# Row maxima of the scores: one unit of each round gets them from ScalarE, and they are spread by DMA instead of TensorE

## The reference

```python
xn = layernorm(x)                                   # x is 4 x 1024 x 256
q, k, v = split_heads(xn @ Wq), *split(xn @ Wkv)    # 16 heads of 64
q, k = rope(q), rope(k)                             # on the first 32 of 64
sim = einsum('bhid,bhjd->bhij', q, k) * 64 ** -0.5
attn = softmax(sim, axis=-1)
out = einsum('bhij,bhjd->bhid', attn, v) -> b n (h d)
x = x + (out @ Wout + bout) + ffn(xn)               # ffn: FP4 blocks of 16, silu(gate) * up, down
```

## Time and profile before

| | |
|---|---|
| median of 3 runs | 1926.34 us (1925.79 to 1928.39) |
| profiled execution | 1927.98 us |
| its span, first to last instruction | 1926.2 us |
| TensorE busy | 1843.6 us, 96% |
| VectorE busy | 1482.3 us, 77% |
| ScalarE busy | 808.2 us, 42% |
| GpSimd busy | 1395.9 us, 72% |

### The profile page before, as it was taken

How to read it: one execution, slowest core, us unless ns; L and a number is a source line. 1 busy time by engine, 2 the same in 40 slices (tenths; PEclk the granted TensorE clock), 3 DMA queues, 4 the chain that set the end, 5 groups by cost and what they waited for, 6 DMA issues and landing times.

```text
span 1926.2 us, 29651 instructions
## 1 busy us (share of the span) xinstructions
PE 1843.6 (96%) x11172; PEld 1147.6 (60%) x11172; DVE 1482.3 (77%) x2032; ACT 808.2 (42%) x1078; POOL 1395.9 (72%) x688
## 2 busy tenths in 40 slices
PE   6989999959999999999999999999999999999989
PEld 5768999835555555555555555555555555555589
DVE  7969999887777777777777777777777777776254
ACT  4642333214444444444444444444444444444432
POOL 4764554407888888888888888888888888889900
PEclk9999999969999999999999999999999999999989
DMA  8550311110221131222223121221322112211474
GB/s 287 234 192 28 127 46 53 42 50 23 53 69 54 54 102 53 65 56 60 63 57 110 53 59 53 61 60 53 90 76 64 58 54 59 53 51 48 148 263 170
DMA packets 151423, 161.33 MB, mean 84 GB/s; under 512 B 43376, under 2 KB 107760, under 8 KB 151024
## 3 DMA queue, kind: packets, MB, share of 16 engines
q1 hardware_dynamic: 151280, 159.43, 26.3%
HBM read 100.14 MB, written 59.24 MB: 83 GB/s over the span
## 4 chain that ended last, share of the span: by engine, by line
PE 63%; DVE 21%; issue 6%; DMA 1%; POOL 1%; ACT 0%; SPq 0%; POOLq 0%; DVEq 0%
PE banks L1005 19%; PE banks L1025 13%; PE banks L948 11%; PE banks L982 9%; PE banks L1008 6%; DVE half_max L1079 3%; PE banks L1516 2%; DVE q_lo L1124 2%; DVE k_lo L1124 2%; PE banks L1034 2%; DVE h_scales L110 2%; DVE f_y L131 2%; DVE f_amax L109 1%; DVE f_y L134 1%; DVE h L583 1%
## 5 line engine op out<-in xcount | busy, mean ns | idle before, releaser
L1203 POOL TENSOR_TENSOR acc<-acc,prob 128x1024 f32<-128x1024 f32 x384 | 917.9, 2390 | 131.2 <-ACT prob L1242 102.3
L1079 DVE TENSOR_REDUCE half_max<-banks 128x2 f32<-128x1024 f32 x512 | 627.2, 1226 | 270.9 <-PE banks L982 270.9
L1242 ACT ACTIVATE prob<-banks 128x1024 f32<-128x1024 f32 x512 | 511.8, 1024 | 633.8 <-PE banks L1008 633.8
L1025 PE MATMUL banks<-prob,v 128*64 128x512 f32 x2048 | 495.7, 605 | 0.0
L1025 PEld LDWEIGHTS banks<-prob,v 128*64 128x64 f32 x2048 | 124.3, 136 | 238.6 <-issue 190.9
L1203 POOL TENSOR_TENSOR acc<-prob,prob 128x1024 f32<-128x1024 f32 x64 | 153.5, 2399 | 124.6 <-ACT prob L1242 124.6
L982 PE MATMUL banks<-k_hi,q_hi 64*128 64x512 f32 x1024 | 230.9, 450 | 12.1 <-DVE half_max L1079 11.0
L948 PE MATMUL banks<-xT,wqk 128*128 128x512 f32 x768 | 218.0, 420 | 3.5 <-DVE k_lo L1124 2.1
L1005 PE MATMUL banks<-q_hi,k_lo 64*128 64x512 f32 x1024 | 202.9, 393 | 0.0
L1008 PE MATMUL banks<-max_rows,ones_r 64*128 64x512 f32 x1024 | 202.8, 392 | 0.0
L1005 PE MATMUL banks<-q_hi,k_hi 64*128 64x512 f32 x1024 | 202.4, 392 | 0.0
(11 more groups left out here) (121 smaller groups left out, 2152.1 us busy)
## 6 DMA issues: line engine op xcount, KB each, us to landing
v_scratch<-v_out SPq DMA_DIRECT2D x32, 512.0 KB, 2.6
wqk<-wp_scratch SPq DMA_DIRECT2D x32, 512.0 KB, 3.6
v<-v_scratch SPq DMA_DIRECT2D x32, 512.0 KB, 4.7
inv_rows<-inv_scratch SPq DMA_DIRECT2D x128, 128.0 KB, 3.2
o_scratch<-o_norm SPq DMA_DIRECT2D x64, 256.0 KB, 2.1
o_in<-o_scratch SPq DMA_DIRECT2D x8, 2048.0 KB, 11.0
xn_scratch<-p_xT SPq DMA_DIRECT2D x32, 256.0 KB, 3.0
xT<-xn_scratch SPq DMA_DIRECT2D x8, 1024.0 KB, 6.3
```

Of the source, the lines that this page charges most:

```text
L1025: ins = nc.tensor.matmul(o_ps[head * DH:(head + 1) * DH, :], v[s % 2][:, kt, at:at + DH], prob[n % SLOTS][:, head, :], start=kt == 0, stop ...
L1079: nc.vector.tensor_reduce(half_max[:, half % 2, :, t % GRP, part], guess_bank(s, i), axis=AX.X, op=ALU.max, negate=True).then_inc(half_max ...
L1203: nc.gpsimd.tensor_tensor(acc[b][:, :, :], first, prob[n % SLOTS][:, :, :], ALU.add).then_inc(added, 1)
L1242: nc.scalar.activation(prob[n % SLOTS][:, :, :], s_ps[n % 2][:, :, :], ACT.Exp).then_inc(exp_done, 1)
```

## The change

- The transposition of the maxima leaves TensorE. `turn_max` is now VectorE's: a transpose of `max_cols` (now 128x32) in blocks of 32x32, behind `rotate` in rounds 3 and 7. Four small DMAs bring the parts together in DRAM in the order of the queries (`store_max`), and one DMA spreads the 1024 values of a half, both heads, to all 128 partitions of `max_all` (`spread_max`, 512 KB). `spread_rows`, the 0/1 table and its load go.
- Even units keep a pair of products for the maxima, now with a matrix whose row 0 (of each head) is one and whose others are zero, and `max_all` as the moving operand.
- Odd units have no such pair. ScalarE copies `max_all` into their two banks (`seed`) behind the exponential that empties them, and all six products add to what lies there (`start=False`).

```diff
@@ misc_table, begin, tensor @@
-            if r == 0 and 0 <= s < STEPS:
-                job("turn", s, 1)
-            if r == 4 and 0 <= s + 1 < STEPS:
-                job("turn", s + 1, 0)
...
-        elif before == "turn":
-            pe.wait_ge(rows_done, 2 * s + k + 1)
@@ scores @@
+            has_seed = kt % SEEDED_EVERY == 1
+            if has_seed:
+                pe.wait_ge(seeded, n // SEEDED_EVERY + 1)
+            elif n >= 2:
+                pe.wait_ge(exp_done, n - 1)
             if kt == 0:
-                pe.wait_ge(rows_done, 2 * s + half + 1)
-            if n >= 2:
-                pe.wait_ge(exp_done, n - 1)
-            elif n == 1:
-                pe.wait_ge(kept["h_high"], TILES)
+                pe.wait_ge(max_in[half], 16 * (s + 1))
...
-                    nc.tensor.matmul(s_ps[n % 2][:, head, :], left[rows, keys], right[rows, queries], start=k == 0, stop=False)
-            for head in range(2):
-                rows = slice(head * DH, (head + 1) * DH)
-                ins = nc.tensor.matmul(s_ps[n % 2][:, head, :], ones_r[rows, :], max_rows[half][rows, :], start=False, stop=True)
+                    ins = nc.tensor.matmul(s_ps[n % 2][:, head, :], left[rows, keys], right[rows, queries],
+                                           start=k == 0 and not has_seed, stop=k == 2 and has_seed, skip_group_check=has_seed)
+            if not has_seed:
+                for head in range(2):
+                    rows = slice(head * DH, (head + 1) * DH)
+                    ins = nc.tensor.matmul(s_ps[n % 2][:, head, :], first_row[rows, :], max_all[half][rows, head, :], start=False, stop=True)
@@ vector @@
-        def spread_rows(s, half):
-            dve.wait_ge(misc_done, job["turn", s, half] + 1)
...
+        def turn_max(s, half):
+            dve.wait_ge(max_done, 2 * s + half + 1)
             if s:
-                dve.wait_ge(scored, (s - 1) * UNITS + (half + 1) * QT)
-            nc.vector.tensor_tensor(max_rows[half][:, :].rearrange("p (t n) -> p t n", t=GRP),
...
+                dve.wait_ge(max_stored[half], 16 * QUAD * s)
+            nc.vector.transpose(max_turned[half][:, :].bitcast(F32), max_cols[half][:, :].bitcast(F32)).then_inc(max_turn, 1)
@@ the loop of vector @@
+                if r in (3, 7) and scoring(s + 1):
+                    turn_max(s + 1, r // 4)
@@ scalar @@
+        def seed(n):
+            s, u = divmod(n, UNITS)
+            if u % QT == 1:
+                act.wait_ge(max_in[u // QT], 16 * (s + 1))
+            if n == 1:
+                act.wait_ge(half_maxed, UNITS)
+            else:
+                act.wait_ge(exp_done, n - 1)
+            nc.scalar.activation(s_ps[n % 2][:, :, :], max_all[u // QT][:, :, :].bitcast(F32), ACT.Copy).then_inc(seeded, 1)
...
                     exponent(s * UNITS + 2 * r + 1)
+                    if s * UNITS + 2 * r + 3 < STEPS * UNITS:
+                        seed(s * UNITS + 2 * r + 3)
+                elif s == -1 and r == ROUNDS - 1:
+                    seed(1)
@@ sync @@
+        def store_max(s, half):
+            if s:
+                sp.wait_ge(max_in[half], 16 * s)
+            sp.wait_ge(max_turn, 2 * s + half + 1)
+            for k in range(QUAD):
+                sp.dma_start(io["max_scratch"][half, :, :, k * QROWS:(k + 1) * QROWS].rearrange("h t c -> (h t) c"),
+                             max_turned[half][k * QROWS:k * QROWS + 2 * GRP, :].bitcast(F32)).then_inc(max_stored[half], 16)
+        def spread_max(s, half):
+            sp.wait_ge(max_stored[half], 16 * QUAD * (s + 1))
+            if s:
+                sp.wait_ge(scored, (s - 1) * UNITS + (half + 1) * QT)
+            sp.dma_start(max_all[half][:, :, :].rearrange("p h c -> p (h c)").bitcast(F32),
+                         io["max_scratch"][half].rearrange("h t p -> (h t p)").partition_broadcast(P)).then_inc(max_in[half], 16)
@@ the loop of sync @@
+            if scoring(s):
+                store_max(s, 1)
             if scoring(s - 1):
                 spread_inverse(2 * (s - 1))
+            if scoring(s):
+                spread_max(s, 1)
...
                 store_o(2 * (s - 1))
+            if scoring(s + 1):
+                store_max(s + 1, 0)
+                spread_max(s + 1, 0)
             if scoring(s - 1):
                 spread_inverse(2 * (s - 1) + 1)
```

More of the change, by code:

```diff
@@ L836 @@
 HALVES = 2 * STEPS
+SEEDED_EVERY = 2
 def attention_part(nc, zones, banks, sem, io, kept, output):
@@ L851, in attention_part @@
     shuffled = [first(f"shuffled{i}", [P, GCOL], F32) for i in range(2)]
-    own = small("own", [P, GRP], F32)
     ones = small("ones", [P, QROWS], F32)
-    ones_r = small("ones_r", [P, P], F32R)
+    first_row = small("first_row", [P, P], F32R)
     half_max = small("half_max", [P, 2, 2, GRP, 2], F32)
-    max_cols = [small(f"max_cols{i}", [P, P], F32) for i in range(2)]
-    max_rows = [small(f"max_rows{i}", [P, GCOL], F32R) for i in range(2)]
+    max_cols = [small(f"max_cols{i}", [P, QROWS], F32R) for i in range(2)]
+    max_turned = [small(f"max_turned{i}", [P, QROWS], F32R) for i in range(2)]
     compact = small("compact", [P, 2, 2, GRP], F32)
@@ L869, in attention_part @@
     o_norm = [late(f"o_norm{i}", [P, GCOL], F32) for i in range(2)]
+    max_all = [late(f"max_all{i}", [P, 2, GCOL], F32R) for i in range(2)]
     bout = late("bout", [P, D], F32)
@@ L884, in attention_part @@
     res_stored, wp_stored, down_done = kept["res_stored"], kept["wp_stored"], kept["down_done"]
-    guessed, half_maxed, max_done, rows_done = sem("guessed"), sem("half_maxed"), sem("max_done"), sem("rows_done")
+    guessed, half_maxed, max_done, seeded = sem("guessed"), sem("half_maxed"), sem("max_done"), sem("seeded")
+    max_turn = sem("max_turn")
+    max_stored, max_in = [sem(f"max_stored{i}") for i in range(2)], [sem(f"max_in{i}") for i in range(2)]
     scored, exp_done, pv_done, added = kept["scored"], sem("exp_done"), kept["pv_done"], kept["added"]
@@ L1036, in column_sums @@
             ins.then_inc(misc_done, 1)
-        def turn_max(s, half):
-            begin(pe, "turn", s, half)
-            pe.wait_ge(max_done, 2 * s + half + 1)
-            nc.tensor.transpose(misc_ps[:, 0:P], max_cols[half][:, :], ident[:, :]).then_inc(misc_done, 1)
-        pe.wait_ge(cleared, 4)
+        pe.wait_ge(cleared, 6)
         for s in range(-2, STEPS + 1):
@@ L1064, in tensor @@
                     column_sums(s, 0)
-                if r == 0 and scoring(s):
-                    turn_max(s, 1)
-                if r == 4 and scoring(s + 1):
-                    turn_max(s + 1, 0)
     def vector(dve):
@@ L1131, in invert @@
             nc.vector.reciprocal(inv_compact[:, b, :, :], compact[:, b, :, :]).then_inc(inv_done, 1)
-        dve.wait_ge(cleared, 4)
-        dve.wait_ge(tables_in, 32)
+        dve.wait_ge(cleared, 6)
+        dve.wait_ge(tables_in, 16)
         rotate(0, K0)
@@ L1145, in vector @@
                     maximum(s + 1, 2 * r)
-                if r == 1 and scoring(s):
-                    spread_rows(s, 1)
-                if r == 5 and scoring(s + 1):
-                    spread_rows(s + 1, 0)
                 if r == 0 and scoring(s + 1) and s >= 0:
@@ L1402, in clear @@
     def clear(dve):
-        nc.vector.memset(max_cols[0][:, :], 0.0).then_inc(cleared, 1)
-        nc.vector.memset(max_cols[1][:, :], 0.0).then_inc(cleared, 1)
+        nc.vector.memset(max_cols[0][:, :].bitcast(F32), 0.0).then_inc(cleared, 1)
+        nc.vector.memset(max_cols[1][:, :].bitcast(F32), 0.0).then_inc(cleared, 1)
         nc.vector.memset(ones[:, :], 1.0).then_inc(cleared, 1)
-        nc.vector.memset(ones_r[:, :].bitcast(F32), 1.0).then_inc(cleared, 1)
+        nc.vector.memset(first_row[:, :].bitcast(F32), 0.0).then_inc(cleared, 1)
+        dve.wait_ge(cleared, 4)
+        for head in range(2):
+            nc.vector.memset(first_row[head * DH:head * DH + 1, :].bitcast(F32), 1.0).then_inc(cleared, 1)
     def first_loads(sp):
@@ L1414, in first_loads @@
         load_x(sp, 0, 1)
-        sp.dma_start(own[:, :], io["tables"][:, P + 2 * SEQ:]).then_inc(tables_in, 16)
         load_wqk(sp, 1)
@@ L1641, in shape_constants @@
             turn[head * DH + dim, 1] = sin[:, dim // 2] if dim % 2 == 0 else -sin[:, dim // 2]
-    own = (np.arange(P)[:, None] % DH == np.arange(GRP)[None, :]).astype(np.float32)
-    return np.concatenate([np.eye(P, dtype=np.float32), turn.reshape(P, 2 * SEQ), own], 1)
+    return np.concatenate([np.eye(P, dtype=np.float32), turn.reshape(P, 2 * SEQ)], 1)
 def kernel(L0_attn_queries, L0_attn_Wq, L0_attn_Wkv, L0_attn_Wout, L0_attn_bout, L0_ffn_w_gate, L0_ffn_w_up, L0_ffn_w_down):
@@ L1677 @@
     io["sum_scratch"] = nc.dram_tensor("sum_scratch", (2, 2, GCOL), F32).ap()
+    io["max_scratch"] = nc.dram_tensor("max_scratch", (2, 2, GRP, P), F32).ap()
     io["inv_scratch"] = nc.dram_tensor("inv_scratch", (2, 2, GCOL), F32).ap()
```

4 lines of the change are left out of this document (1 added, 3 removed).

## The result

The changed kernel takes **1844.01 us**, the median of 4 runs (1841.81 to 1845.23), against 1926.07 us (1924.23 to 1928.39) of the kernel before, run beside it: a ratio of 0.957, 95% interval 0.956 to 0.959. The forecast was 1845, from 1838 to 1872. The profiled execution took 1844.23 us with a span of 1842.5, so the span shrank by 83.7 us.

A forecast was written before the change was run, and what follows sets the result against it. TensorE, busy 199.04 of 200 us, and its turns with DVE bound attention. Thirty steps of 2.64 us (79.2) and 1.9 at the start gave −81: 1927.98 to 1846.9, forecast 1845 after the 1.64 offset from the median, range 1838 to 1872.

The forecast's parts named there:

- Max products of odd units: On TensorE, eight pairs a step dropped at 0.2325 us each: 1.86 us a step saved.
- the tie: Round 0: the second guess's result reaches DVE at 2.40 us, the rotary addition frees DVE at 2.38: just in time.
- The turn: In rounds 0 and 4, values to next guess fall from 2.25 to 1.86 us: 0.39 twice, 0.78 us a step.
- Seeds: ACT copies into two score banks, 1.02 us each, with 0.42 us spare in round 0: cost nothing.
- B: Late seeds: writing two banks takes 2.05 us, rounds 0 and 4 lose 0.67 each, 40 us, 1885; chance 0.06.
- Rival C: DVE's transpose in rounds 3 and 7 waits for POOL's addition, at 2.38 us losing 134 us, 1979; chance 0.05.
- DMA: Added stores and loads cost nothing; second half's spread lands by 15 us, seed issued about 18: thinnest cover some 3.
- POOL: Some 38 us a step, room within 40.96; it bounds the last two steps, so 30 steps count: 79.2 us.
- The start: DVE idles 1.30 us for guesses behind the first turn and spends 0.60 on the first spreading: 1.9 us saved.
- A: DVE holds the second guess; in rounds 2 and 6 the pair's time becomes a wait: 14 us, 1859; chance 0.15.
- step 5: DVE's block transpose in rounds 3 and 7, taken as 0.2 us, costs nothing; at 0.73 us it would cost 15 us.
- D: The pair's time on PE only moves into a wait for the seed; 25 us gained, 1901; chance 0.04.

## Why the prediction was right

1. *Max products of odd units*: 8 × 0.2325 = 1.86 a step; the runs without seeds and with the turn show 1.86 and 1.88. The second guess came at T0 + 1.96 (1.97), and DVE was free for its maximum just in time (1005.46, no idle time). That the tie would hold was right; the next pair taken off brings 0.02 us a round and not 0.23.
2. *The turn*: 0.39 twice; 0.38 to 0.39 measured, from the values to the guess 1.87 (1.86).
3. *Seeds*: 1.03 us for 1.02 taken, spare 0.43 for 0.42. Of writing PSUM costing twice an exponential (B) nothing was seen; what it would have cost was undersized, 40 us by the prediction against some 57 in the additions' frame of the doubled seed (1361.8), since neither a wait's aftermath nor rounds 2 and 6 were in it.
4. *Even units*: the pair kept its 0.23.
5. *Transpose*: 0.19 for 0.2; idle 0.27 left of 0.35. Rival C was weighed with a wrong reading: the trace of the kernel before does have instructions of DVE that were held so. Of its 32 multiplications L111 of the feed-forward part, 20 start with POOL idle and take 0.185 to 0.190 us; the other 12 start while POOL works, take 1.20 to 2.29 us and end 0.04 us behind the end of POOL's instruction, as the copies do.

```profile
L111 DVE TENSOR_SCALAR f_inv<-h_scales x32: 185/186/2287, 145.6 to 373.3; 128x44 f32<-128x44 f32 x32
```

   They could have raised C's 0.05; whether a block transpose is held only the changed kernel could tell.
6. *DMA*: lands at 13.5 (by 15), needed at 18.2: cover 4.8 for 3.
7. *POOL*: the step 40.94 for 40.96; 30 steps × 2.64 = 79.2 against 78.4. In steps of 2.64 that is 29.7. Where the 0.8 us went is not shown; POOL's new gap of 2.37 us near the end is a place where some of it could be.
8. *The start* was the weakest term: 1.9 us forecast, 5.0 seen. Of these 1.8 lie ahead of all changed work (the first 8-column reduction starts at 411.54 instead of 413.32) and belong to how one execution differs from the next: in the ten other kernels of the experiments, which all share the change up to there, that reduction starts anywhere from 411.39 to 414.70. The other 3.2 are 1.3 more than forecast. Most of that is the spreading of the maxima, which had been counted with its 0.60 us on DVE. The projection behind the first turn uses the same bank and waited 1.50 us for it (L948 at 422.62, 9.30 us behind that reduction; now L945 at 418.03, 6.49 behind its own). DVE's next rotary multiplication comes 12.27 us behind the reduction before, 10.76 with the turn alone put back and 9.45 in the changed kernel: the turn is worth 1.3 there and the spreading 1.5. The last 0.4 us stay open.

The sum came out closer than its terms. The profiled executions differ by 83.7 us of span for 81.1 worked out, that is 0.8 less in the steps, 3.1 more ahead of them, of which 1.8 is no effect of the change, and 0.3 behind them; the medians differ by 82.1. Part of the match of 1844.01 with 1845 is luck. The upper end of the range is A's 1859 and the 15 us of step 5, which make 1874 and not 1872.

Rival A was right about the mechanism and wrong about the place by one pair; B had its place right and its price too low, as the doubled seed shows; C is true of the copy and not of the transpose; D was refuted by the seedless kernel.

## What to carry to other kernels

Where a product only adds a known term to a PSUM bank, an engine with idle time can write that term first and the products go on top; cost it at the product's full time, and look at the engine's queue for the latest point at which it may be done. In every kernel here a product with `start=True` had written each of these places before the first seed (the first step's guesses in banks 0 and 1), and none with `start=True` stood between a seed and its products; whether the sum comes out without the former no run here shows. When two engines arrive together, the next thing taken off one of them is worth little, so work out how much room the partner has before taking off more. A wait on TensorE is to be costed with about 0.11 us on top of its length, even one of almost no length.

## What was not expected of the hardware

- A score product that had to wait, if only for some hundredths, or that follows products of another shape, shows 0.50 us and not 0.39, and its follower starts 0.34 behind it and not 0.23 (a guess that waited: 0.44 to the values and not 0.32). In the kernels with more seeds and with doubled seeds it is the wait, in the one with later sums the change of shape; each time it is a good part of what the expectation missed.
- ACT writes two PSUM banks from SBUF in 1.029 us, nearly as fast as an exponential the other way, 1.023.
- Block transposes of 128x32 behind one another start 0.093 us apart; one alone lasts 0.19. A plain copy of that shape takes 0.138 us with POOL idle; one that starts while POOL adds ends 0.04 us behind the addition, and the longest took 2.156 us. The block transpose is not held so.
